# Two blocks in one kernel: the order in which GpSimd scatters the picks of the last two sequences

## The reference

```
logits = flat @ router_w.T
scores = jnp.sqrt(jax.nn.softplus(logits))
_, idx = jax.lax.top_k(scores + expert_bias, K)            # K = 4 of 32
topv = topv / (topv.sum(axis=-1, keepdims=True) + 1e-20)
out  = sum over experts of probs[:, e] * clamped_swiglu(flat, expert e)
out  = out + clamped_swiglu(flat, shared expert)
```

## Time and profile before

| what | value |
|---|---|
| median of 3 timed runs | 607.91 us (606.37 to 610.05) |
| span of the profiled execution, first to last instruction | 624.5 us |
| time of the profiled execution beside its span | not given apart from it; the span is 16.6 us above the median |
| busy: TensorE matmul / VectorE / ScalarE / GpSimd | 88% / 69% / 55% / 39% |
| mean granted TensorE clock | 0.967 |
| scatters into `xs` (L922) | 64, 987 ns each, 334 to 453 us |
| scatters into `ys` (L982) | 80, 966 ns each, 459 to 602 us |

### The profile page before, as it was taken

The page is one execution under the profiler, slowest core; times in us unless marked ns, Lnnn a source line. Parts: engine busy times, 40 slices in busy tenths (PEclk is TensorE's granted clock), DMA queues, the critical chain, the costliest instruction groups (busy, mean ns, idle before and its releaser), DMA issues.

```text
span 624.5 us, 14114 instructions
## 1 busy us (share of the span) xinstructions
PE 550.5 (88%) x4231; PEld 390.9 (63%) x4232; DVE 433.0 (69%) x1298; ACT 346.5 (55%) x898; POOL 241.2 (39%) x341
## 2 busy tenths in 40 slices
PE   9998799999879989989998888866589999989996
PEld 4665455665458754666666665534367787778775
DVE  5678858888147886677788683535667777778755
ACT  3533657776826578456675456513146565656672
POOL 2533000000153213266544435556735555555530
PEclk9999979999999999999999899778799999999998
DMA  8599707000680005766505162235545454445498
GB/s 252 179 304 331 211 1 207 3 3 3 192 219 1 2 1 166 209 206 183 229 19 206 62 229 71 70 137 219 170 126 140 140 159 144 151 135 154 143 396 328
DMA packets 49554, 95.24 MB, mean 153 GB/s; under 512 B 8596, under 2 KB 40540, under 8 KB 46940
## 3 DMA queue, kind: packets, MB, share of 16 engines
q1 hardware_dynamic: 41820, 75.34, 39.4%
q0 software_dynamic: 7680, 19.21, 8.2%
HBM read 58.54 MB, written 35.59 MB: 151 GB/s over the span
## 4 chain that ended last, share of the span: by engine, by line
PE 54%; DVE 20%; issue 9%; ACT 6%; DMA 4%; POOL 3%; another core or an unknown queue 2%; SPq 1%; DVEq 0%; ACTq 0%; POOLq 0%
PE banks L1731 7%; PE banks L1513 6%; PE banks L1469 5%; PE banks L1322 4%; PE banks L1742 4%; PE banks L1534 4%; DVE mx L2087 3%; DVE mx L2090 3%; PE banks L1399 3%; PE banks L1794 2%; PE banks L1328 2%; DMA arena<-negT 2%; PE banks L1720 2%; DMA pvs<-rows_by_expert 2%
## 5 line engine op out<-in xcount | busy, mean ns | idle before, releaser
L1162 ACT ACTIVATE arena<-banks 128x512 f32<-128x512 f32 (+1 forms) x256 | 130.1, 550 | 83.3 <-PE banks L1513 45.8
L982 POOL DMA_INDIRECT results_by_rank<-attn_w,goes x80 | 77.3, 966 | 72.2 <-issue 47.9
L1513 PE MATMUL banks<-arena 98*128 98x256 bf16 (+1 forms) x512 | 88.6, 267 | 15.9 <-DVE arena L2186 3.8
L2087 DVE TENSOR_REDUCE mx<-banks 128x4 f32<-128x1024 f32 x64 | 76.0, 1220 | 18.1 <-PE banks L1469 18.0
L922 POOL DMA_INDIRECT rows_by_expert<-arena,bpb x64 | 63.2, 987 | 57.6 <-ACT arena L1162 22.4
L1469 PE MATMUL banks<-arena 96*128 96x256 bf16 (+1 forms) x512 | 81.5, 263 | 4.2 <-DVE mx L2087 2.5
L1731 PE MATMUL banks<-arena,attn_w 128*128 x320 | 84.4, 387 | 0.3 <-issue 0.3
L1513 PEld LDWEIGHTS banks<-arena 98*128 98x128 bf16 x512 | 43.2, 100 | 49.7 <-ACT arena L1162 15.0
L2090 DVE TENSOR_REDUCE mx<-banks 128x4 f32<-128x1024 f32 (+1 forms) x48 | 57.7, 1221 | 22.3 <-PE banks L1473 20.2
L1469 PEld LDWEIGHTS banks<-arena 96*128 96x128 bf16 x512 | 49.9, 99 | 20.0 <-issue 6.0
L1731 PEld LDWEIGHTS banks<-arena,attn_w 128*128 128x128 f32 x320 | 55.6, 194 | 5.1 <-issue 0.7
(11 more groups left out here) (253 smaller groups left out, 1095.7 us busy)
## 6 DMA issues: line engine op xcount, KB each, us to landing
arena<-parts_dram SPq DMA_DIRECT2D x72, 256.0 KB, 4.1
pvs<-rows_by_expert SPq DMA_DIRECT2D x80, 130.0 KB
parts_dram<-arena SPq DMA_DIRECT2D x24, 384.0 KB, 4.8
arena<-results_by_rank SPq DMA_DIRECT2D x6, 1024.0 KB, 10.3
arena<-in SPq DMA_DIRECT2D x2, 2304.0 KB
rows_by_expert<-zero SPq DMA_DIRECT2D x1, 4160.0 KB, 23.6
arena<-in SPq DMA_DIRECT2D x2, 1920.0 KB
arena<-in SPq DMA_DIRECT2D x3, 768.0 KB
```

Of the source, the lines that this page charges most:

```text
L982: pool.indirect_dma_start(ys, bass.IndirectOffsetOnAxis(ap=goes[:, j % 4:j % 4 + 1], axis=0), yb[j % 4], None).then_inc(y_stored[j % 4], 16)
L1162: act.activation(p_ring[n][:, i % P_RING, :], st_bank[RING_AT[n]["s", b, s] % 3][:, 0:P_WIDTH[n]], ACT.Exp, scale=HD ** -0.5).then_inc(exp ...
L1513: ins = pe.matmul(dst[:, at:at + SEQ - q0], keys, q_rows(n, slice(0, ROWS), s, b, q0, SEQ - q0), start=True, stop=(n == 0 or b < POOL_MASKS))
L2087: ins = dve.tensor_reduce(out, src.rearrange("p (q h k) -> p q h k", q=QT, k=nk), AX.X, ALU.max)
```

## The change

The sixteen scatters of sequences 6 (batch 3) and 7 (batch 4) are issued in another order. Before: picks 3 and 2 of sequence 6, picks 3 and 2 of sequence 7, then pick 1 of both, then pick 0 of both. After: all four picks of sequence 6, then all four of sequence 7. `scatter_picks(j, ...)` begins with the wait for batch j's row numbers. Nothing else differs.

```diff
@@ -963,11 +963,8 @@
             scale_rows(7)
             for t, k in tiles[4:]:
                 scatter(t, k)
-            scatter_picks(3, (3, 2))
-            scatter_picks(4, (3, 2))
-            for k in (1, 0):
-                scatter_picks(3, (k,))
-                scatter_picks(4, (k,))
+            scatter_picks(3, (3, 2, 1, 0))
+            scatter_picks(4, (3, 2, 1, 0))
             pool.wait_ge(placed[0], 2 * TILES * 16)
             pool.wait_ge(picks_placed, 2)
             pool.nop().then_inc(picks_placed, 1)
```

## The result

The changed kernel takes 609.73 us (median of 22 runs, 607.1 to 612.27), the kernel before 606.18 us (22 runs, 600.67 to 610.14). The ratio is 1.0065, with a 95% interval of 1.0049 to 1.0082: 3.9 us slower, between 3.0 and 5.0. The forecast was no change. The time itself lies in the range of 605.2 to 610.6 us, but by luck: the range was set around 607.91 us, the median of three runs, and 22 runs give 606.18 us for the same kernel. The direction was not foreseen.

A forecast was written before the change was run, and what follows sets the result against it. It read the path as VectorE's block tables, SyncE's sequencer, one block load, then TensorE, without GpSimd in the changed stretch. All terms summed to 0, with +0.7 and -0.4 as ends: 607.9 us, range 605.2 to 610.6.

The forecast's parts named there:

- (a): GpSimd's scatters: sixteen before and after, 0.96 us each, 1.26 us start to start; no instruction added or removed.
- (b): GpSimd's order: four scatters fill its idle 3.15 us, delay sequence 7's start by 2.21 us, and end 3.15 us sooner.
- (c): Level 3, first needed by block 7: comes at 451.6 instead of 454.7, already 4.8 us early; worth 0.
- (d): Level 1 at SyncE's first load: second pick-3 scatter 2.21 us later, level at 444.2, asked at 445.0; cost 0, worst 0.7 us.
- (e): Level 2 at SyncE's block 3 load: comes between 446.5 and 448.2, needed after 450; cost 0.
- (f): ScalarE's shared tanh and block 0 copy queued behind the level waits: 1.3 us to spare or 0.4 us late; taken as 0.
- (g): GpSimd's first result scatter behind level 3 waits for ScalarE until 459.25 anyway; cost 0.
- (h): Up to four more scatters meet the experts' weights in the DMA queues: 0.53 MB, 1.4 us, hidden.
- R1: Late level 1 at SyncE and level 2 at ScalarE slow the kernel by 0.7 to 2.2 us; chance 0.12.
- R2: Level 3 gates block 7's load at SyncE, so up to 3.15 us come back: 604.8 us; chance 0.04.
- R3: SyncE's slow 0.7 us steps end with GpSimd's scatters, saving at most 1.8 us: 606.1 us; chance 0.07.
- R4: TensorE's clock rises at another time, 1.8 us either way: 606.1 or 609.7 us; chance 0.05.

The follow-up runs named there:

- second profile: The kernel before, unedited, profiled again: this execution took 604.02 us with a span of 602.2 us; ratio to before 1.001 (0.9987 to 1.0033).
- 9: Kernel before, same scatter order, with 18 unused VectorE additions ahead of handing over sequence 7's row numbers: 612.51 us, ratio 1.0098.
- 10: Changed kernel's scatter order with 18 unused VectorE additions ahead of handing over sequence 7's row numbers: 612.46 us, ratio 1.0094 to the kernel before.
- Kernel 2: Against the kernel before, only sequence 7's pick 2 comes late, behind all of sequence 6 and pick 3: ratio 1.005, +3.0 us (1.8 to 4.3).
- 4: Kernel before with ScalarE's wait for level 2 put behind the last shared tanh and block 0's copy: ratio 1.0017, +1.0 us (-0.7 to 2.8).
- 7 to 10: First: kernel before, block 0 copied ahead of the last shared tanh, ratio 1.0002; second: also scatters by pick, 1.0017; last two: late row numbers, 1.0098 and 1.0094.

## Why the prediction was wrong

**The frame.** The prediction saw that the span of 624.5 us stood 16.6 us above the timed median, and then worked in its times and carried the difference over unchanged. The order of two events decided the sign, GpSimd's end with its first four scatters of sequence 6 and VectorE's row numbers. In the profiled execution GpSimd was 3.15 us early. In the second profile it is late: its fourth scatter ends at 420.62 + 0.96 = 421.58, 1.3 us after VectorE starts to hand over. That is the root.

**(a)** right: the same scatters at the same price, 1.26 to 1.27 us each.

**(b)** is the step that failed. Four scatters were to fill an idle 3.15 us and pass on 2.21 us of delay. There is nothing to fill, and the whole 4 x 1.27 = 5.1 us are passed on (421.88 - 420.30 = 1.6 us behind the row numbers before, 427.60 - 420.96 = 6.6 after). The end of the scatters doesn't come sooner.

**(c)** right that level 3 is worth nothing here, for the wrong number: it doesn't come at 451.6 in place of 454.7 but stays. Kernels 9 and 10 show that with row numbers this late even 5 us at level 3 are worth nothing. The margin of 4.8 us was not there either. In the second profile of the kernel before, SyncE's fourth wait for a buffer (block 7's) is over at 439.3, level 3 comes at 439.6, and the load goes out right behind it (lines L760, 415 to 445 us, and L761, 439 to 440 us):

```profile
L760 SPq EVENT_SEMAPHORE  x4: 17/17/17, 434.7 to 439.3; - x4
...
L761 SPq FUSED_REGOPS  x1: 37/37/37, 439.7 to 439.7; - x1
```

TensorE doesn't feel these 0.4 us: it turns block 7 at 442.67 without a wait. In the changed kernel block 7's load follows at 443.9, 4.4 us behind level 3. The counts behind step (c), 338, 411 and 183 rows, are right, but 27 fewer for expert 1 (411 - 384), not over 40, would move a block.

**(d)** failed with (b) and by its margin. Its landing term was right: the second pick-3 scatter needs 431.4 - 428.87 = 2.5 us to level 1, the shorter of the two delays, as chosen. But its margin of 1.6 us was not there. Counted from the row numbers, level 1 is raised at 5.8 us in the first profile and at 6.6 in the second, where GpSimd comes late, and SyncE's load starts at 7.4 (444.95 - 437.53, the handing over in the first profile) and at 6.8 without the slow steps. In the second profile 0.2 us are left, and level 1 moves by 10.4 - 6.6 = 3.8 us where 2.2 less a shorter landing had been reckoned.

**(e)** Level 2 at block 3's load: not separated. In the changed kernel the first gate-and-up starts 1.1 us after level 2 and sets the pace, and block 3's load, issued right behind level 2 at 435.2, is there in time: TensorE turns block 3 at 439.89 without a wait.

**(f)** named the right place and priced it at 0. It reckoned with level 2 at 446.5 - 437.5 = 9 us behind the row numbers, 1.3 us ahead of VectorE's release. It came at 14.2, and the release at 430.57 - 420.30 = 10.3 us covers no more of it than that. Kernel 2 shows this term alone at 3 us. In the sum it also stood as -0.4 us, a gain, where being 0.4 us late is a cost; the range doesn't hang on that.

**(g), (h)** right: GpSimd's first result scatter still waits for ScalarE (5.78 us in the changed kernel, 6.12 in the earlier trace rows), and the weights are not what TensorE waits for.

**The rivals.** R1 is what happened, in both its places, by its own rule (level 1 later than SyncE's request, level 2 later than VectorE's release). It had a chance of 0.12 and a price of 0.7 to 2.2 us; the price was 3.9, since it too rested on a shift of 2.2 us. It even said what was needed, a SyncE without the 0.7 us steps, and I took the steps to be the usual state. R2, that level 3 coming sooner gives time back, did not happen: level 3 didn't come sooner in the changed kernel, and where it did, in 10 against 9, nothing came back. Its condition, that SyncE stands at block 7's wait when level 3 comes, is met in the second profile of the kernel before, by 0.4 us that TensorE doesn't feel. R3 has nothing to act on: without slow steps there is no coupling to see. R4: the clock rises at the same block before and after; the four gate-and-up matmuls take 2.07 and 2.07 us for block 0, 1.52 and 1.36 for block 1, 1.03 and 1.03 for block 2 (second profile of before, changed kernel).

**The rule weighed at (d).** Level 2 moved by 14.2 - 7.9 = 6.3 us, 1.2 more than the four scatters. This is the landing again: from the last pick-2 scatter's start to level 2 it is 3.6 us in the changed kernel (431.52 to 435.15), 2.5 in the kernel before (425.69 to 428.2), 2.9 in kernel 2 (434.68 to 437.56). What the DMA queues moved in the meantime, changed kernel from 431.5 to 435.2 us:

```profile
q1 hardware_dynamic: 432, 0.40, 41.7%
q0 software_dynamic: 140, 0.40, 28.8%
```

and kernel before, second profile, from 425.6 to 428.3:

```profile
q0 software_dynamic: 108, 0.29, 28.9%
q1 hardware_dynamic: 6, 0.01, 2.1%
```

In the changed kernel SyncE's loads of blocks 0 to 2, released by level 1, run beside the scatter that level 2 waits for. By the Trainium skill ("DMA: Bandwidth & Descriptors", section "SWDGE vs HWDGE vs iDMA") the DMA engines take turns between the two kinds of queue, and I had read it as "no added delay". The rows side with the other end, but not for all of the 1.1 us. The scatter at 431.52 is itself busy for 1.30 us in place of 0.96, and so is the one of kernel 2 (1.25 us), whose landing takes 2.9 us with only 0.02 MB on the hardware queue. So 0.3 to 0.4 us go with the longer scatter and 0.7 to 0.8 with the loads beside it. For level 1, whose second scatter takes 0.96 us, the landing beside 0.5 to 0.7 MB of weights is 3.4 to 4.1 us in eight profiles (both of before, kernels 2, 4 and 7 to 10), which is 0.9 to 1.6 us longer than 2.5. That no run isolates, so it is a reading of these windows and not shown by an experiment.

## What to carry to other kernels

Before a margin of 1 to 4 us is read from a profile, compare the profiled execution with the timed ones; if it is longer than all of them, its small gaps and its order of events need not be theirs, and another profile costs little. An engine's idle gap in front of a wait is a place to fill only if it is there in the usual execution; otherwise whatever is put in front delays what stands behind by its full length. When an engine counts arrivals on behalf of others, look at what stands behind that wait in its own queue: here block 0 was held up by rows that it doesn't need.

## What was unexpected of the hardware

The landing of a 128-row scatter follows its start by 2.5 us when the hardware queue is quiet and by 3.4 to 4.1 us beside 0.4 to 0.7 MB of other loads, as worked out above. Of the 64 such scatters of the changed kernel, most take 0.96 us and three take 1.25 to 1.30 us. Each of the other profiles has three or four of over 1.2 us, the longest 1.54 us in kernel 10, and in nine of the twelve one of them is the twelfth of the last sixteen, in whatever order these go (at 431.52 in the changed kernel, 430.84 in the second profile of before); why, I don't know. In one of twelve profiles SyncE's register steps took 0.7 us each for 10 us on end, in the other eleven some 0.04 us.
